# A block of cross attention, self attention and 32 experts on one core: a constant filler operand, the router's root as a power on POOL, and a different split between whole and split weights

## The chip, the core and the metric

The kernel runs on one core of one Trainium2 chip. The metric is the device time of one execution in microseconds. TensorE's matmuls appear as PE in the profile and its weight loads as PEld; VectorE is DVE, ScalarE is ACT, GpSimd is POOL, SyncE is SP.

## The reference

The input x is 4 x 32 rows of 256 numbers, so 128 rows fill the 128 partitions. Three residual steps follow, each on a layer norm of x:

```
x = x + cross_attention(layernorm(x), ctx_512)     # 16 heads, causal: only the first 32 of 512 positions count
x = x + attention(layernorm(x))                    # 16 heads; q, k, v, o are W x + b plus a rank-16 product, scaled 0.5
x = x + experts(layernorm(x))

experts: scores = sqrt(softplus(h @ router_w.T))            # 128 x 32
         idx    = top 4 of scores + expert_bias
         p      = scores at idx, divided by their sum; 0 elsewhere
         out    = sum over 32 experts of p * (silu(clip(h @ gate.T)) * clip(h @ up.T)) @ down.T
                + the same of one shared expert, with weight 1      # clip to -7..7, inner width 128
```

All of it is computed for every expert; the router's weights are zero for those not chosen. Inputs, weights and output are float32.

## The kernel before, in words

The order of every engine's instructions is written out by hand; semaphores join the engines. x stays in one 128 x 256 tile. Attention comes first, in two passes (`a` = 0 and 1), and then the experts in 16 **pairs** of two. Code and text count pairs 0 to 15; the TensorE functions take n = pair + 1, with n = 0 for the shared expert.

**Whole and split.** A product of float32 operands can be done *whole*, directly from the loaded weights (`gate_up_whole`, `down` for n up to `FIRST`). Or it can be done *split*: the weights are written as a high part in a shorter format plus a low part (the remainder), the activations likewise, and TensorE adds three products of high and low parts (`HI_LO`). Gate and up weights of pairs below `WHOLE` are used whole, the others split. Down weights of the last `LAST` pairs are split, the others whole.

**Who makes the parts.** ACT copies the loaded weights (`gu_raw`, eight slots) to the high part in `gu_w` (`gu_high`, L654 to L659, one pair at a time). POOL subtracts it and writes the low part in halves of 128x512 (`gu_low`, L324 to L329). For down weights the same is done by `dn_high` (L742 to L747) and L337 to L341, which put both parts in slots of `gu_w` that are free by then. `gate_up` for a split pair waits for each half's low part (L555). POOL runs one list: three powers for the layer norms' inverse roots (`inverse_sqrt`), two sums for the merged value weights, then the low parts. It waits for the last shift of the second attention (L322) before the first low part, and after four halves for the third inverse root and for the gate (L333 to L335).

**The opening.** TensorE starts with `WARM` = 9 matmuls on a tile of ones (`keep_busy`, L416 to L420), which DVE sets first (L834). Some more of these stand in the attention.

**The router.** From the logits ACT and DVE take absolute value, exponential, logarithm and a ratio to softplus (L714 to L720 and L912 to L920). The square root is then made by ACT as exp(ln / 2) (L723 and L726) and refined by one division and sum on DVE (L927 to L934), so `score2` is twice the root. DVE adds the bias to get the key (L935), finds the top eight, marks the chosen ones, sums and divides (L937 to L942): this is the gate. ACT loads the table for silu behind the exponential (L727). DVE's `clip` of the shared expert and of pair 0 stands between these steps (L923, L929).

**The expert loop** (L613 to L622 on TensorE) does, for n from 2 to 16: `gate_up(n + 4)`, the transposes of n, `down(n - 2)`. DVE clips (L900), ACT applies silu (L734), DVE multiplies with up and the gate (`gate_h`, L953), TensorE transposes, ACT copies (`hT_unit`, L740), and for split downs DVE makes the low part (`hT_low`, L966). ACT has one gu conversion per round.

**Loads.** SP issues nearly all loads in one order (L254 to L285): attention's, gu 4, 5, 6, 0, shared, 1, 2, 3, 7, down 0 to 3, and then gu and down in turn. gu 8 to 11 wait for both low halves of pairs 4 to 7, gu 12 to 15 for TensorE's whole products, since they reuse slots.

Of the kernel before, what the change touches and what calls it, by code (L numbers as in the profile page):

```python
# [12 lines left out]
BF16 = mybir.dt.bfloat16  # L13
# [6 lines left out]
T = B * S  # L20
# [17 lines left out]
WHOLE = 4  # L38
LAST = 6
# [3 lines left out]
TINY = 1e-30  # L43

# [11 lines left out]
def raw_slot(p):  # L56
    return p if p < RAW else (p - WHOLE) % RAW


def build(nc, x, consts, mask, small, ctx_kv, x_wq, lora, rows, attn_w, shared_w, moe_w, out):  # L60
    with ExitStack() as ctx:
# [46 lines left out]
        ln_floor = sb("ln_floor", [T, 1])  # L108
# [20 lines left out]
        warm_sb = sb("warm_sb", [128, 128], BF16)  # L129
# [8 lines left out]
        ln_softplus = sb("ln_softplus", [T, E])  # L138
        half_power = sb("half_power", [T, E])
        root = sb("root", [T, E])  # L140
        inv_root = sb("inv_root", [T, E])
        score2 = sb("score2", [T, E + 1])
# [29 lines left out]
        warm_set = sem("warm_set")  # L172
# [54 lines left out]
        ln_softplus_ready = sem("ln_softplus_ready")  # L227
        half_power_ready = sem("half_power_ready")
        root_ready = sem("root_ready")
# [22 lines left out]
        @block.sync  # L252
        def _(sp):
            for name, dst, src in (("x", x_sb[:], x), ("xwq", xwq_sb[:], x_wq), ("mask", mask_sb[:], mask), ("lora", lora_sb[:], lora),  # L254
                                   ("aw_kq", aw_sb[:, 0:2], attn_w[:, 0:2]), ("small", small_sb[:], small),
                                   ("aw_vo", aw_sb[:, 2:4], attn_w[:, 2:4]), ("rows", bo_rows[:], rows.to_broadcast([T, D]))):
                sp.dma_start(dst, src).then_inc(ld[name], 16)

            def load_gu(p):
                if p >= RAW + WHOLE:  # L260
                    sp.wait_ge(gu_ready, p - RAW - WHOLE + 2)
                elif p >= RAW:
                    for c in range(DC):
                        sp.wait_ge(gu_lo_ready[c], p - RAW + 1)
                sp.dma_start(gu_raw[:, raw_slot(p)], moe_w[:, p * PAIR:p * PAIR + DC * GU]).then_inc(ld_gu[p], 16)

            def load_dn(p):
                sp.dma_start(dn_w[:, p * 2 * D:(p + 1) * 2 * D], moe_w[:, p * PAIR + DC * GU:(p + 1) * PAIR]
                             ).then_inc(ld_dn[p], 16)

            load_gu(WHOLE)
            load_gu(WHOLE + 1)
            load_gu(WHOLE + 2)
            load_gu(0)
            sp.dma_start(shared_sb[:], shared_w).then_inc(ld["shared"], 16)
            for p in range(1, WHOLE):
                load_gu(p)
            load_gu(WHOLE + 3)
            for p in range(WHOLE):
                load_dn(p)  # L280
            for p in range(RAW, PAIRS):
                load_gu(p)
                load_dn(p - RAW + WHOLE)
            for p in range(PAIRS - RAW + WHOLE, PAIRS):
                load_dn(p)  # L285
            sp.wait_ge(fin, 1)
            sp.dma_start(out, x_sb[:]).then_inc(stored, 16)
            sp.wait_ge(stored, 16)

        @block.gpsimd  # L290
        def _(pool):
            nc.gpsimd.memset(minus_mean[:], -1.0 / D).then_inc(powers_set, 1)
            nc.gpsimd.memset(inv_sqrt_power[:], -0.5).then_inc(powers_set, 1)
            nc.gpsimd.memset(ln_floor[:], 2.0 ** -64).then_inc(powers_set, 1)
            nc.gpsimd.memset(v_heads[:], 0.0).then_inc(zeroed, 1)
            nc.gpsimd.memset(key[:, E:E + K], SENTINEL).then_inc(zeroed, 1)
            nc.gpsimd.memset(score2[:, E:E + 1], 2e-20).then_inc(zeroed, 1)
# [46 lines left out]
        def _(pe):  # L344
# [265 lines left out]
            gate_up(WHOLE + 1)  # L610
# [16 lines left out]
        def _(act):  # L627
# [26 lines left out]
            def gu_high(p):  # L654
# [4 lines left out]
                nc.scalar.activation(gu_w[:, p % SLOTS, 0], gu_raw[:, raw_slot(p)], ACT.Copy).then_inc(gu_hi_ready, 1)  # L659
# [21 lines left out]
            gu_high(WHOLE)  # L681
            act.wait_ge(xt_psum, 1)
# [17 lines left out]
            gu_high(WHOLE + 1)  # L700
# [3 lines left out]

            act.wait_ge(xt_psum, 3)
# [5 lines left out]
            nc.scalar.activation(xnT_parts[:, 0], xfT[:], ACT.Copy).then_inc(xt_hi_ready, 1)  # L711
            act.wait_ge(rstd_ready[2], 1)
# [8 lines left out]
            act.wait_ge(softplus_ready, 1)  # L721
            act.wait_ge(powers_set, 3)
# [43 lines left out]
        def _(dve):  # L766
# [67 lines left out]
            nc.vector.memset(warm_sb[:], 1.0).then_inc(warm_set, 1)  # L834
# [73 lines left out]
            for w, bound in enumerate((CLIP, -CLIP)):  # L908
# [8 lines left out]
            step(nc.vector.tensor_tensor(den[:], den[:], e_abs[:], ALU.mult))  # L917
# [20 lines left out]
            step(nc.vector.match_replace(replaced[:], top8[:], key[:], -SENTINEL))  # L938
            step(nc.vector.scalar_tensor_tensor(weight[:], replaced[:, 0:E + 1], -SENTINEL, score2[:],
# [104 lines left out]
```

## Time and profile before

| | |
|---|---|
| time of the runs | 74.11, 76.31, 76.15 us; median 76.15 |
| profiled execution | 74.17 us, its span 72.2 us |
| PE / PEld busy | 67.5 us / 49.4 us |
| DVE, ACT, POOL busy | 44.7, 40.9, 42.9 us |
| bytes read from HBM | 15.52 MB |

The span runs from the first to the last instruction of the profiled execution; the time of an execution has a little more around it. The views used below are the page's busy line, its groups of instructions, the chain of waits in order of time, the timeline, and the DMA issues of a window with their time to landing. Times in the timeline and in the chain are counted from the span's start.

### The profile page before, as it was taken

What the parts mean: (1) busy time and instruction counts of PE and PEld (TensorE: products, weight loads), DVE (VectorE), ACT (ScalarE), POOL (GpSimd) and SP (SyncE); (2) the same over time, 40 slices, a digit from 0 to 9 for tenths busy, and PEclk for the clock granted to TensorE, in tenths of its full rate; (3) what the DMA queues carried; (4) which work ended last, traced back from release to release, by engine and by line L of the source; (5) the groups of instructions that cost most, each with busy time, mean ns of one, the idle gap of its engine ahead of it and who ended that gap; (6) DMA issues with size and microseconds to landing.
All of it is one profiled execution on the core that took longest, in us unless ns stands there. A gap on an engine that the chain in (4) does not pass through costs nothing.

```text
span 72.2 us, 1555 instructions
## 1 busy us (share of the span) xinstructions
PE 67.5 (93%) x552; PEld 49.4 (68%) x552; DVE 44.7 (62%) x126; ACT 40.9 (57%) x88; POOL 42.9 (59%) x50
## 2 busy tenths in 40 slices
PE   4999998999999999999999999999999999998950
PEld 1337565797864495644686888887888888897940
DVE  0058587684697627598999936634753574589520
ACT  0604556375449440459969968868960366696300
POOL 7330006150009973000799999999999999999200
PEclk9999999999999999999999999999999999999999
DMA  0899999999999499800006999999990000000002
GB/s 5 276 295 267 375 331 378 390 417 417 412 402 386 161 265 315 328 15 5 0 0 159 318 354 385 397 395 415 382 365 25 9 0 0 0 0 0 0 0 73
DMA packets 6342, 15.74 MB, mean 218 GB/s; under 512 B 704, under 2 KB 1472, under 8 KB 6336
## 3 DMA queue, kind: packets, MB, share of 16 engines
q1 hardware_dynamic: 6048, 15.39, 59.5%
q10 hardware_dynamic: 288, 0.27, 1.1%
q8 instruction: 4, 0.07, 0.3%
q14 instruction: 2, 0.02, 0.1%
HBM read 15.52 MB, written 0.13 MB: 217 GB/s over the span
## 4 chain that ended last, share of the span: by engine, by line
PE 68%; DVE 15%; ACT 9%; issue 4%; POOL 1%; DVEq 0%; ACTq 0%
PE bP L557 15%; PE bY L579 11%; PE bE L419 6%; PE bXT L569 5%; PE bP L356 4%; PE bY L587 4%; PE bE L557 4%; DVE gu_clip L900 3%; PE bY L408 3%; PE bXT L412 3%; PE bP L383 2%; DVE h L953 2%; DVE shifted L795 2%; ACT L727 2%; DVE row_max L793 2%
## 5 line engine op out<-in xcount | busy, mean ns | idle before, releaser
L328 POOL TENSOR_TENSOR gu_w<-gu_raw,gu_w 128x512 fp32r<-128x512 f32 x24 | 29.9, 1281 | 11.5 <-DVE gate L942 6.0
L557 PE MATMUL bP<-gu_w,xnT_parts 128*128 128x512 f32 x60 | 17.6, 428 | 0.0
L900 DVE TENSOR_SCALAR gu_clip<-bP,clip_at 128x512 f32<-128x512 f32 x13 | 10.4, 808 | 7.7 <-PE bP L557 7.7
L659 ACT ACTIVATE gu_w<-gu_raw 128x1024 fp32r<-128x1024 f32 x12 | 12.7, 1055 | 3.0 <-DMA gu_raw<-moe_w_dram 2.9
L557 PEld LDWEIGHTS bP<-gu_w,xnT_parts 128*128 128x128 f32 x60 | 11.2, 188 | 2.7 <-issue 0.5
L579 PE MATMUL bY<-dn_w,hT 128*128 128x256 f32 x40 | 10.3, 380 | 0.0
L953 DVE SCALAR_TENSOR_TENSOR h<-gu_clip,gate,bP 128x128 f32<-128x128 f32 x26 | 7.8, 340 | 0.5 <-ACT bP L734 0.4
L340 POOL TENSOR_TENSOR gu_w<-dn_w,gu_w 128x512 fp32r<-128x512 f32 x6 | 7.5, 1276 | 0.0
L579 PEld LDWEIGHTS bY<-dn_w,hT 128*128 128x128 f32 x40 | 6.8, 190 | 0.5
L740 ACT ACTIVATE hT<-bXT 128x256 f32<-128x256 f32 (+1 forms) x11 | 4.0, 366 | 4.8 <-PE bXT L569 4.8
L569 PE MATMUL bXT<-consts_sb,h 128*128 128x128 f32 x33 | 6.3, 275 | 0.3 <-DVE hT_parts L966 0.2
L734 ACT ACTIVATE bP<-gu_clip,rstd 128x256 f32<-128x256 f32 x13 | 6.1, 471 | 0.0
L569 PEld LDWEIGHTS bXT<-consts_sb,h 128*128 128x128 f32 x33 | 4.3, 140 | 2.5 <-DVE h L953 0.9
L419 PE MATMUL bE<-warm_sb 128*128 128x512 bf16 x12 | 5.0, 569 | 1.0 <-DVE warm_sb L834 1.0
L543 PE MATMUL bP<-gu_raw,xfT 128*128 128x512 f32 x12 | 5.7, 599 | 0.0
L316 POOL TENSOR_TENSOR aw_sb<-aw_sb,lora_v 128x256 f32<-128x256 f32 x2 | 1.4, 730 | 6.4 <-ACT lora_v L651 6.4
L587 PE MATMUL bY<-gu_w,hT_parts 128*128 128x256 f32 x36 | 5.2, 289 | 0.0
L308 POOL TENSOR_TENSOR rstd<-var_eps,inv_sqrt_power 128x1 f32<-128x1 f32 x3 | 1.8, 599 | 5.5 <-DVE var_eps L780 5.5
L587 PEld LDWEIGHTS bY<-gu_w,hT_parts 128*128 128x128 f32 x36 | 4.5, 189 | 0.0
L788 DVE TENSOR_TENSOR k_heads<-bP,consts_sb 128x512 f32<-128x512 f32 x4 | 2.7, 689 | 2.1 <-PE bP L426 1.1
L900 DVE TENSOR_SCALAR gu_clip<-bE,clip_at 128x512 f32<-128x512 f32 x3 | 2.4, 807 | 2.3 <-PE bE L557 2.3
L740 ACT ACTIVATE hT_parts<-bXT 128x256 fp32r<-128x256 f32 x6 | 2.3, 380 | 2.5 <-PE bXT L569 2.5
(151 smaller groups left out, 105.8 us busy)
## 6 DMA issues: line engine op xcount, KB each, us to landing
gu_raw<-moe_w_dram SPq DMA_DIRECT2D x16, 512.0 KB, 9.0
dn_w<-moe_w_dram SPq DMA_DIRECT2D x16, 256.0 KB, 8.2
aw_sb<-attn_w_dram SPq DMA_DIRECT2D x2, 512.0 KB, 7.1
shared_sb<-shared_w_dram SPq DMA_DIRECT2D x1, 384.0 KB, 12.3
small_sb<-small_dram SPq DMA_DIRECT2D x1, 370.0 KB, 7.0
xwq_sb<-x_wq_dram SPq DMA_DIRECT2D x1, 256.0 KB, 3.5
lora_sb<-lora_dram SPq DMA_DIRECT2D x1, 256.0 KB, 4.4
ctx_sb<-ctx_kv_dram ACTq DMA_DIRECT2D x1, 192.0 KB, 3.0
```

Source lines behind the costliest of these rows:

```text
L328: nc.gpsimd.tensor_tensor(gu_w[:, p % SLOTS, 1, cols], gu_raw[:, raw_slot(p), cols], gu_w[:, p % SLOTS, 0, cols], ALU.subtract).then_inc(g ...
L340: nc.gpsimd.tensor_tensor(dn_part(i, 1), dn_w[:, at:at + 2 * D], dn_part(i, 0), ALU.subtract).then_inc(dn_lo_ready, 1)
L419: nc.tensor.matmul(bank, warm_sb[:], warm_sb[:].unsqueeze(1).to_broadcast([128, 4, 128]), start=True, stop=True, skip_group_check=True)
L557: last = nc.tensor.matmul(bGU[n % 5][:, 0:GU], xnT_parts[:, a, k, :], gu_w[:, (n - 1) % SLOTS, w, k * GU:(k + 1) * GU], start=(k == 0 and ...
L569: last = nc.tensor.transpose(bHT[n % 2][:, e * T:(e + 1) * T], h[:, n % 4, e, :], ident)
L579: last = nc.tensor.matmul(bY[:, 0:D], hT[:, n % 3, e, :], dn_w[:, at:at + D], start=False, stop=False, skip_group_check=True)
L587: last = nc.tensor.matmul(bY[:, 0:D], hT_parts[:, n % 3, a, e, :], dn_part(i, w)[:, e * D:(e + 1) * D], start=False, stop=(n == PAIRS and ...
L659: nc.scalar.activation(gu_w[:, p % SLOTS, 0], gu_raw[:, raw_slot(p)], ACT.Copy).then_inc(gu_hi_ready, 1)
L734: nc.scalar.activation(dst, gu_clip[:, n % 4, 0:width, 0, :], ACT.Silu, scale=rstd[:, 2:3]).then_inc(silu_ready, 1)
L740: nc.scalar.activation(dst, bHT[n % 2][:, 0:width * T], ACT.Copy).then_inc(hT_ready, 1)
L900: nc.vector.tensor_scalar(gu_clip[:, n % 4, 0:width], bank[:, 0:width * 2 * I], clip_at[:, 0:1], clip_at[:, 1:2], ALU.min, ALU.max).then_i ...
L953: last = nc.vector.scalar_tensor_tensor(h[:, n % 4, e], gu_clip[:, n % 4, e, 1, :], weight_e, bank[:, e * 2 * I:e * 2 * I + I], ALU.mult, ...
```

## The change

Five things change.

1. The filler matmuls take constants that the program has anyway (a column of ones, broadcast) in place of the tile that DVE set.
2. The root is one `pow` with exponent 0.5 on POOL. ACT's second logarithm and second exponential and DVE's half_power, reciprocal, product and sum go. `score` is the root itself, not twice the root. POOL's wait for the gate stands right behind it.
3. `WHOLE` goes from 4 to 2: pairs 2 and 3 are split too. ACT makes the high parts of pairs 2 to 6 and one half of pair 7 ahead of the router, some in halves (`gu_high_chunk`). POOL doesn't wait for the shift any more and does nine halves, not four, before the third inverse root. In the loop ACT is one conversion further ahead (`EARLY` = 9).
4. `LAST` goes from 6 to 8: eight down products are split.
5. SP's order of loads changes; the `rows` load moves behind two gu loads.

```
-WHOLE = 4
-LAST = 6
+WHOLE = 2
+EARLY = 9
+LAST = 8
+SMALLEST = 2e-38
 def raw_slot(p):
-    return p if p < RAW else (p - WHOLE) % RAW
+    return p if p < RAW else (p + WHOLE) % RAW
...
+        ones = nc.const_aps.tensor(1.0, [128, 128], BF16)
+        ones_wide = nc.const_aps.tensor(1.0, [128, 512], BF16)
...
@@ SP: loads
-                if p >= RAW + WHOLE:
-                    sp.wait_ge(gu_ready, p - RAW - WHOLE + 2)
+                if p >= 2 * RAW - WHOLE:
+                    sp.wait_ge(gu_ready, p - 2 * RAW + WHOLE + 2)
...
             load_gu(WHOLE)
             load_gu(WHOLE + 1)
-            load_gu(WHOLE + 2)
+            sp.dma_start(bo_rows[:], rows.to_broadcast([T, D])).then_inc(ld["rows"], 16)
+            for p in range(WHOLE + 2, RAW - 1):
+                load_gu(p)
             load_gu(0)
+            load_gu(RAW - 1)
             sp.dma_start(shared_sb[:], shared_w).then_inc(ld["shared"], 16)
-            for p in range(1, WHOLE):
+            load_gu(1)
+            for p in range(RAW, RAW + 4):
+                load_dn(p - RAW)
                 load_gu(p)
-            load_gu(WHOLE + 3)
-            for p in range(WHOLE):
+            for p in range(4, 8):
                 load_dn(p)
-            for p in range(RAW, PAIRS):
+            for p in range(2 * RAW - WHOLE, PAIRS):
                 load_gu(p)
-                load_dn(p - RAW + WHOLE)
-            for p in range(PAIRS - RAW + WHOLE, PAIRS):
+            for p in range(RAW + 4, 2 * RAW - WHOLE):
+                load_gu(p)
+            for p in range(8, PAIRS):
                 load_dn(p)
@@ POOL
-            pool.wait_ge(shift_ready, 2 * DC)
             def gu_low(p, c):
-                pool.wait_ge(gu_hi_ready, p - WHOLE + 1)
+                pool.wait_ge(gu_hi_ready, DC * (p - WHOLE) + c + 1)
...
-                    if (p, c) == (WHOLE + 2, 0):
+                    if (p, c) == (WHOLE + 4, 1):
                         inverse_sqrt(2)
+                        pool.wait_ge(softplus_ready, 1)
+                        nc.gpsimd.tensor_tensor(score[:, 0:E], softplus[:], half[:], ALU.pow).then_inc(score_ready, 1)
                         pool.wait_ge(gate_ready, 1)
@@ TensorE
-                    nc.tensor.matmul(bank, warm_sb[:], warm_sb[:].unsqueeze(1).to_broadcast([128, 4, 128]),
+                    nc.tensor.matmul(bank, ones, ones_wide,
...
-            pe.wait_ge(warm_set, 1)
...
             pe.wait_ge(xt_lo_ready, 1)
-            gate_up(WHOLE + 1)
+            for n in range(WHOLE + 1, 6):
+                gate_up(n)
@@ ACT
+            def gu_high_chunk(p, c):
+                act.wait_ge(ld_gu[p], 16)
+                cols = slice(c * GU, (c + 1) * GU)
+                nc.scalar.activation(gu_w[:, p % SLOTS, 0, cols], gu_raw[:, raw_slot(p), cols], ACT.Copy
+                                     ).then_inc(gu_hi_ready, 1)
             gu_high(WHOLE)
+            gu_high_chunk(WHOLE + 1, 0)
             act.wait_ge(xt_psum, 1)
             nc.scalar.activation(xcT[:, 0], bXT0[:, 0:T], ACT.Copy).then_inc(xt0_ready, 1)
...
+            gu_high_chunk(WHOLE + 1, 1)
...
+            gu_high(WHOLE + 2)
             exp_half(1, 0)
...
             copy_probsT(1)
-            gu_high(WHOLE + 1)
+            gu_high(WHOLE + 3)
...
+            gu_high_chunk(WHOLE + 4, 0)
...
+            gu_high_chunk(WHOLE + 4, 1)
+            gu_high_chunk(WHOLE + 5, 0)
             act.wait_ge(rstd_ready[2], 1)
...
-            nc.scalar.activation(ln_softplus[:], softplus[:], ACT.Ln, bias=ln_floor[:]
-                                 ).then_inc(ln_softplus_ready, 1)
-            act.wait_ge(half_power_ready, 1)
-            nc.scalar.activation(root[:], half_power[:], ACT.Exp, scale=0.5).then_inc(root_ready, 1)
             nc.scalar.preload_act_table(ACT.Silu)
...
-            gu_high(WHOLE + 2)
+            gu_high_chunk(WHOLE + 5, 1)
             silu_unit(0)
             silu_unit(1)
-            gu_high(WHOLE + 3)
+            for p in range(WHOLE + 6, EARLY + 1):
+                gu_high(p)
...
-                if n + 3 + WHOLE < PAIRS:
-                    gu_high(n + 3 + WHOLE)
+                if EARLY + n < PAIRS:
+                    gu_high(EARLY + n)
@@ DVE
-            nc.vector.memset(warm_sb[:], 1.0).then_inc(warm_set, 1)
...
-            step(nc.vector.tensor_tensor(den[:], den[:], e_abs[:], ALU.mult))
+            step(nc.vector.scalar_tensor_tensor(den[:], e_abs[:], SMALLEST, den[:], ALU.max, ALU.mult))
...
-            dve.wait_ge(ln_softplus_ready, 1)
-            nc.vector.scalar_tensor_tensor(half_power[:], logits_sb[:], -100.0, ln_softplus[:], ALU.max, ALU.min
-                                           ).then_inc(half_power_ready, 1)
             clip(1)
-            dve.wait_ge(root_ready, 1)
-            step(nc.vector.reciprocal(inv_root[:], root[:]))
-            step(nc.vector.tensor_tensor(inv_root[:], inv_root[:], softplus[:], ALU.mult))
             dve.wait_ge(zeroed, 3)
-            step(nc.vector.tensor_tensor(score2[:, 0:E], inv_root[:], root[:], ALU.add))
-            step(nc.vector.scalar_tensor_tensor(key[:, 0:E], score2[:, 0:E], 0.5, small_sb[:, EBIAS:EBIAS + E],
-                                                ALU.mult, ALU.add))
+            dve.wait_ge(score_ready, 1)
+            step(nc.vector.tensor_tensor(key[:, 0:E], score[:, 0:E], small_sb[:, EBIAS:EBIAS + E], ALU.add))
```

## Rows read from the trace of the kernel before

**Rows 1.** The page's busy time, share of the span and instructions of each engine.

```profile
PE 67.5 (93%) x552; PEld 49.4 (68%) x552; DVE 44.7 (62%) x126; ACT 40.9 (57%) x88; POOL 42.9 (59%) x50
```

**Rows 2.** Chain of waits, opening and router: start us, us, what.

```profile
1.04 4.02 PE bE L419 x9
...
31.59 0.14 DVE half_power L927
...
32.00 1.28 ACT L727
```

**Rows 3.** Timeline, opening: start us, us, engine, line, operation [idle before, releaser].

```profile
0.82 0.17 DVE L834 MEMSET warm_sb<- 128x128 bf16 x1 [0.82 <-PEq L1037]
```

**Rows 4.** Timeline of the router stretch, DVE and POOL.

```profile
27.80 0.15 DVE L780 TENSOR_SCALAR var_eps<-moments 128x1 f32<-128x1 f32 x1
...
30.95 0.19 DVE L920 SCALAR_TENSOR_TENSOR softplus<-logits_sb,ratio 128x32 f32<-128x32 f32 x1
...
31.63 0.81 DVE L900 TENSOR_SCALAR gu_clip<-bP,clip_at 128x512 f32<-128x512 f32 x1
...
33.19 0.19 DVE L935 SCALAR_TENSOR_TENSOR key<-score,small_sb 128x32 f32<-128x32 f32 x1
...
34.76 24.97 POOL L328 TENSOR_TENSOR gu_w<-gu_raw,gu_w 128x512 fp32r<-128x512 f32 x20 [6.05 <-DVE gate L942]
```

**Rows 5.** Timeline, TensorE's weight loads around the first pairs, and POOL's last parts.

```profile
31.23 0.19 PEld L543 LDWEIGHTS bP<-gu_raw,xfT 128*128 128x128 f32 x1 [0.24 <-issue]
...
32.95 0.19 PEld L543 LDWEIGHTS bE<-gu_raw,xfT 128*128 128x128 f32 x1 [0.24 <-issue]
...
38.45 0.20 PEld L569 LDWEIGHTS bXT<-consts_sb,h 128*128 128x128 f32 x2 [0.51 <-DVE h L953]
...
59.69 7.49 POOL L340 TENSOR_TENSOR gu_w<-dn_w,gu_w 128x512 fp32r<-128x512 f32 x6
```

**Rows 6.** Chain of waits, the first expert round and the end.

```profile
39.33 1.41 PE bP L557 x6
40.73 0.22 PE bXT L569 x2
40.95 0.86 PE bY L579 x4
...
63.59 1.15 ACT gu_w L746 x2
...
66.63 0.71 PE bY L587 x6
...
67.55 2.12 PE bY L587 x18
```

**Rows 7.** Timeline of the second half of attention, POOL, ACT and DVE.

```profile
15.88 0.38 POOL L320 TENSOR_SCALAR bo_centred<-consts_sb,bo_mean 128x2 f32<-128x2 f32 x1
...
15.98 0.28 ACT L683 ACTIVATE xcT<-bXT 128x128 f32<-128x128 f32 x1 [0.43 <-PE bXT L486]
...
16.63 0.42 DVE L867 TENSOR_TENSOR xnT<-xcT,bY 128x256 f32<-128x256 f32 x1
...
20.74 0.42 ACT L636 ACTIVATE probs<-shifted 128x256 f32<-128x256 f32 x1 [1.18 <-DVE shifted L795]
...
22.93 1.05 ACT L659 ACTIVATE gu_w<-gu_raw 128x1024 fp32r<-128x1024 f32 x1
```

**Rows 8.** The page's groups: POOL's subtractions, sums and powers | busy us, mean ns | idle before.

```profile
L328 POOL TENSOR_TENSOR gu_w<-gu_raw,gu_w 128x512 fp32r<-128x512 f32 x24 | 29.9, 1281 | 11.5 <-DVE gate L942 6.0
...
L316 POOL TENSOR_TENSOR aw_sb<-aw_sb,lora_v 128x256 f32<-128x256 f32 x2 | 1.4, 730 | 6.4 <-ACT lora_v L651 6.4
...
L308 POOL TENSOR_TENSOR rstd<-var_eps,inv_sqrt_power 128x1 f32<-128x1 f32 x3 | 1.8, 599 | 5.5 <-DVE var_eps L780 5.5
```

**Rows 9.** DMA issues at 4.46 and 5.28 us: KB, us from issue to landing.

```profile
gu_raw<-moe_w_dram SPq DMA_DIRECT2D x1, 512.0 KB, 10.0
...
gu_raw<-moe_w_dram SPq DMA_DIRECT2D x1, 512.0 KB, 10.5
```

More of the change, by code:

```diff
@@ L107, in build @@
         inv_sqrt_power = sb("inv_sqrt_power", [T, 1])
-        ln_floor = sb("ln_floor", [T, 1])
         xc = sb("xc", [T, D])
@@ L128, in build @@
         heads_outT = sb("heads_outT", [128, 2, DC, T])
-        warm_sb = sb("warm_sb", [128, 128], BF16)
+        ones = nc.const_aps.tensor(1.0, [128, 128], BF16)
+        ones_wide = nc.const_aps.tensor(1.0, [128, 512], BF16)
         logits_sb = sb("logits_sb", [T, E])
@@ L137, in build @@
         softplus = sb("softplus", [T, E])
[L138 to L142, printed above, removed]
+        half = sb("half", [T, E])
+        score = sb("score", [T, E + 1])
         key = sb("key", [T, E + K])
@@ L171, in build @@
         powers_set = sem("powers_set")
-        warm_set = sem("warm_set")
         xc_psum = sem("xc_psum")
@@ L226, in build @@
         softplus_ready = sem("softplus_ready")
-        ln_softplus_ready = sem("ln_softplus_ready")
-        half_power_ready = sem("half_power_ready")
-        root_ready = sem("root_ready")
+        score_ready = sem("score_ready")
         route_step = sem("route_step")
@@ L255, in _ @@
                                    ("aw_kq", aw_sb[:, 0:2], attn_w[:, 0:2]), ("small", small_sb[:], small),
-                                   ("aw_vo", aw_sb[:, 2:4], attn_w[:, 2:4]), ("rows", bo_rows[:], rows.to_broadcast([T, D]))):
+                                   ("aw_vo", aw_sb[:, 2:4], attn_w[:, 2:4])):
                 sp.dma_start(dst, src).then_inc(ld[name], 16)
             def load_gu(p):
-                if p >= RAW + WHOLE:
-                    sp.wait_ge(gu_ready, p - RAW - WHOLE + 2)
+                if p >= 2 * RAW - WHOLE:
+                    sp.wait_ge(gu_ready, p - 2 * RAW + WHOLE + 2)
                 elif p >= RAW:
@@ L293, in _ @@
             nc.gpsimd.memset(inv_sqrt_power[:], -0.5).then_inc(powers_set, 1)
-            nc.gpsimd.memset(ln_floor[:], 2.0 ** -64).then_inc(powers_set, 1)
+            nc.gpsimd.memset(half[:], 0.5).then_inc(powers_set, 1)
             nc.gpsimd.memset(v_heads[:], 0.0).then_inc(zeroed, 1)
             nc.gpsimd.memset(key[:, E:E + K], SENTINEL).then_inc(zeroed, 1)
-            nc.gpsimd.memset(score2[:, E:E + 1], 2e-20).then_inc(zeroed, 1)
+            nc.gpsimd.memset(score[:, E:E + 1], 1e-20).then_inc(zeroed, 1)
             pool.wait_ge(zeroed, 3)
@@ L658, in gu_high @@
                     act.wait_ge(gu_ready, p - SLOTS + 2)
-                nc.scalar.activation(gu_w[:, p % SLOTS, 0], gu_raw[:, raw_slot(p)], ACT.Copy).then_inc(gu_hi_ready, 1)
+                nc.scalar.activation(gu_w[:, p % SLOTS, 0], gu_raw[:, raw_slot(p)], ACT.Copy).then_inc(gu_hi_ready, DC)
+            def gu_high_chunk(p, c):
[3 more added lines that the diff above has]
+                                     ).then_inc(gu_hi_ready, 1)
             for c, done in ((0, xc0_ready), (1, xc1_ready)):
@@ L720, in _ @@
             nc.scalar.activation(ln_one_plus[:], one_plus[:], ACT.Ln).then_inc(ln_ready, 1)
-            act.wait_ge(softplus_ready, 1)
-            act.wait_ge(powers_set, 3)
-            nc.scalar.activation(ln_softplus[:], softplus[:], ACT.Ln, bias=ln_floor[:]
-                                 ).then_inc(ln_softplus_ready, 1)
-            act.wait_ge(half_power_ready, 1)
-            nc.scalar.activation(root[:], half_power[:], ACT.Exp, scale=0.5).then_inc(root_ready, 1)
             nc.scalar.preload_act_table(ACT.Silu)
@@ L923, in _ @@
             clip(0)
-            dve.wait_ge(ln_softplus_ready, 1)
-            nc.vector.scalar_tensor_tensor(half_power[:], logits_sb[:], -100.0, ln_softplus[:], ALU.max, ALU.min
-                                           ).then_inc(half_power_ready, 1)
             clip(1)
-            dve.wait_ge(root_ready, 1)
-            step(nc.vector.reciprocal(inv_root[:], root[:]))
-            step(nc.vector.tensor_tensor(inv_root[:], inv_root[:], softplus[:], ALU.mult))
             dve.wait_ge(zeroed, 3)
-            step(nc.vector.tensor_tensor(score2[:, 0:E], inv_root[:], root[:], ALU.add))
-            step(nc.vector.scalar_tensor_tensor(key[:, 0:E], score2[:, 0:E], 0.5, small_sb[:, EBIAS:EBIAS + E],
-                                                ALU.mult, ALU.add))
+            dve.wait_ge(score_ready, 1)
+            step(nc.vector.tensor_tensor(key[:, 0:E], score[:, 0:E], small_sb[:, EBIAS:EBIAS + E], ALU.add))
             step(nc.vector.max(top8[:], key[:]))
             step(nc.vector.match_replace(replaced[:], top8[:], key[:], -SENTINEL))
-            step(nc.vector.scalar_tensor_tensor(weight[:], replaced[:, 0:E + 1], -SENTINEL, score2[:],
+            step(nc.vector.scalar_tensor_tensor(weight[:], replaced[:, 0:E + 1], -SENTINEL, score[:],
                                                 ALU.is_equal, ALU.mult, accum_out=weight_sum[:, 0:1]))
```

## Prediction

> **What bounds the kernel now.** I read the page's busy line first: TensorE is busy 67.5 of 72.2 us, POOL 42.9 [rows 1]. Shares over a whole span do not say what an edit is worth, so the chain of waits is read next, stretch by stretch.
>
> Opening: nine filler matmuls take 4.02 us of the chain, and the first real matmul comes right behind them [rows 2]. They do 512 columns in 4.02/9 = 0.447 us each, the 1.2 GHz level. The first waits for a DVE set that starts at 0.82 and holds the filler back until 1.04 [rows 2, 3].
>
> Router: the variance is formed at 27.80, softplus starts at 30.95, the key at 33.19, and POOL, which waits for the gate, takes up its low parts at 34.76 [rows 4]. The chain here goes through the root's steps and ACT's table load of 1.28 us [rows 2]. From 34.76 on POOL never pauses: 20 low parts in 24.97 us, then 6 for down weights until 67.18 [rows 4, 5]. TensorE stands still once, up to 0.5 us ahead of the transposes at 38.45, for DVE's h [rows 5].
>
> Experts: from 39.33 TensorE repeats 1.40 us (gate and up of a split pair), 0.22 (transposes) and 0.86 (an unsplit down), 2.48 in all; a split down takes 0.71 [rows 6]. DVE and ACT wait for it. Ten such rounds (24.8), four transpose steps and six split downs (4 x 0.22 + 6 x 0.71 = 5.14) would end at 69.27; the last matmul ends at 69.67 [rows 6]. The 0.40 of stall lie behind two conversions on ACT at 63.59 that hold back the last silus [rows 6]. POOL's last product is there at 67.18, 1.8 us before the last down starts (69.67 - 0.71 = 68.96): POOL has slack now.
>
> **The change, part by part.** The sum is against the profiled execution: 72.2 us of span, 74.17 us of time, 1.97 us around it.
>
> *Opening.* The DVE set goes; the constant it is replaced by is written before the program's own work. TensorE can start where DVE did, at 0.82 instead of 1.04: 0.22 us. Above, 0.3; below, nothing: if the clock rises when it does now, the first products merely run at the slow level. I take 0.20.
>
> *Conversions in attention.* Pairs 2 to 6 and half of 7 are now made high by ACT ahead of the router, in pieces: a whole one 1.05 us [rows 7], a half 1.15/2 = 0.58, like a down weight of its size [rows 6]. The first half needs the second gu load. The first two landed at 4.46 + 10.0 = 14.46 and 5.28 + 10.5 = 15.8 [rows 9]; the 128 KB of rows no longer stand ahead, a quarter of the 1.3 us between them, so 15.5 now. The half ends near 16.1; the copy to xcT (15.98, less 0.20, by itself) then runs 16.1 to 16.4, just before xnT's start at 16.63 - 0.20 = 16.43 [rows 7]. Cost nothing, at worst 0.3 if the load is as late as the second is now. The tightest of the other places is a whole conversion of 1.05 in the 1.18 us that ACT waits before its exponential at 20.74 [rows 7]; what does not fit there comes straight onto the chain.
>
> *POOL in attention.* Its wait for the shift goes. It is free at 15.88 + 0.38 - 0.20 = 16.1 [rows 7] and does nine low parts before the third root, at 24.97/20 = 1.248 us each [rows 4]: 11.2 us, and pair 5's parts can't start before 22.93 + 1.05 - 0.20 = 23.8 [rows 7], where the seventh part would stand at 23.6. So the ninth ends at 27.5. The variance is ready at 27.80 + 0.15 - 0.20 = 27.75: the third root is not late, by 0.2 us. Cost nothing.
>
> *Root.* Removed: ACT's logarithm and exponential, and on DVE half_power, a reciprocal and the products around it; added: one power on POOL, 128x32. DVE now goes softplus, clip 0, clip 1, key. Clip 1 starts at 31.63 less half_power's 0.14 [rows 2] less 0.20 = 31.29 and takes 0.81 [rows 4]: the key can start at 32.10 instead of 33.19, **1.09 us earlier**. POOL can start the power at 31.0 (softplus ends at 31.14 - 0.20). So a power of up to 1.0 us is hidden behind the two clips. Its price: the trace has only 128x1, 0.60 us; a plain 128x256 costs 0.73 and a 128x512 1.28 [rows 8], which is 2.15 ns a column and 0.18 fixed. Lower end 0.60 + 31 x 0.00215 = 0.67. Upper end, if all over 0.18 is paid per column: 0.18 + 32 x 0.42 = 13.6. I take at most 1.0, since 32 columns of the same operation are nearer to its row of one column than to a cost that grows thirty-twofold. It is the weakest step, and both ends are kept.
>
> The Trainium skill (GPSIMD Engine Reference, section Elementwise, side-by-side cycle accounting) puts a two-input element at about 2.6 cycles, which the 2.15 ns bear out, and data-dependent branching at about 12 cycles an element at 1.2 GHz. By that the power would be 0.60 + 0.32 = 0.9 us, an estimate from that page, and the time the forecast's; by the rows' upper end it would be the slower rival's.
>
> *Table load.* It goes ahead of softplus on ACT, which has then nothing to do until clip 0 is through. The 1.28 us leave the chain.
>
> *Two pairs split instead of whole.* A whole pair takes 1.72 us (weight loads at 31.23 and 32.95 begin two of them [rows 5]), a split one 1.40: 0.64 off TensorE. It was ready for the transposes of 2 at 38.45 - 0.51 = 37.94 [rows 5]; now at 37.94 - 0.20 - 0.64 = 37.10. h comes with the gate, at 38.45 - 1.09 = 37.36. A stall of 0.3 stays, and 1.09 us are gained here, the three parts together.
>
> *Two more down products split.* 2 x (0.86 - 0.71) = 0.30 off TensorE. ACT's last conversions now fall in round 11, ahead of the last silus, so the 0.40 of stall goes. TensorE's end: 69.67 - 1.09 - 0.30 - 0.40 = 67.88.
>
> *What is late next.* POOL has 28 + 8 = 36 parts instead of 30; nine are done before the gate, 27 stand behind it where 26 did. It starts at 34.76 - 1.09 = 33.67 and ends at 33.67 + 27 x 1.248 = 67.37; the last down is 0.71 more, with 0.05 for the signal: **68.13**. That is later than 67.88, so POOL sets the end. Gain 69.67 - 68.13 = 1.5 us.
>
> *DMA.* gu loads 8 to 11 wait for low parts that are done between 18.6 and 26.4 and are sent while the queue is still full; 14 and 15 wait for products that are through at 31.2 [rows 5]; 12 waits for the tenth part, 34.9, and is converted some 5 us later. In the queue the down loads 0 to 7 now come earlier, 8 to 15 last, for products after 50 us. Cost nothing, covered by several us.
>
> Sum: 74.17 - 1.5 = **72.6 us**, 2.1% less. The median of the runs shown, 76.15, lies 1.98 over the profiled execution (the lowest, 74.11, with it). A median of the new kernel that fell as high would be 74.6.
>
> **Rivals.**
> *The power costs more than its cover, in part.* Each us over 1.0 moves gate, h and POOL's 27 parts alike: at 2.0 us 73.6, at 2.5 the gain is gone. For it: one column costs 0.42 over a plain one. Against: that may be fixed. 0.23.
> *The power is paid per column: slower.* Place: POOL between softplus and key. It decides from 2.5 us on, beyond 2% from 4.0 us. At the upper end of 13.6 us the gate comes 12.6 later: 85.2 us. Against it: that a loop over 32 columns would overlap nothing. 0.13.
> *A cover in attention fails,* or the opening brings nothing: the first half, the conversion before the exponential or the third root late by 0.2 to 0.6 us: about 73.1. For it: margins of 0.0 to 0.2. 0.13.
> *More than forecast.* The opening gives 0.3 and POOL's parts follow closer, so that TensorE sets the end: 67.8, time 72.3 or below. 0.06.
> The forecast itself, 72.3 to 72.9: 0.45.
>
> **How the numbers follow.** About 2% (1.5 us) is what a measurement can tell from no change; faster is below 72.7. The forecast straddles it, more below than above (0.34), the last rival adds 0.06, the first 0.02: 0.42. Same: the rest of the forecast, most of the first rival, the third: 0.46. Slower 0.12. The range goes from 71.8 (TensorE's end and the opening's unknowns) to 75.0, which holds a power of up to 3.4 us and a median at 74.6; the dear power stays out.
>
> **What would show it.** First filler at 0.8; xnT at 16.4; nine low parts from 16.1 to 27.5, third root at 27.8; power at most 1.0 us, key at 32.1, POOL's next part at 33.7; transposes of 2 at 37.4; rounds of 2.48 without a gap; POOL's last part at 67.4 and the last six matmuls behind it. A power over 1 us, a third root after 28, or gaps on TensorE between 40 and 60 us would make it wrong.

## The result: 4.3% slower, and the profile after

The changed kernel takes 77.76 us in the median of five runs (76.74 to 79.17), the kernel before 74.11 (73.70 to 76.31, also five runs; the three listed ahead are among them). In some executions of every kernel here the time is about 3 or 7% longer (the changed kernel's profiled one, 79.17 us, is such a one), and the ratios leave these out. The ratio is **1.043, interval 1.037 to 1.049**. The forecast was 72.6 us, in a range up to 75.0; slower had a chance of 0.12.

The page's busy line, to set beside [rows 1]:

```profile
PE 70.0 (91%) x558; PEld 52.8 (68%) x560; DVE 44.3 (57%) x123; ACT 43.7 (57%) x93; POOL 55.8 (72%) x57
```

POOL is busy 12.9 us more. Six more low parts are 6 x 1.25 = 7.5; the other 5.4 are one instruction. The page's groups of POOL, to set beside [rows 8]:

```profile
L328 POOL TENSOR_TENSOR gu_w<-gu_raw,gu_w 128x512 fp32r<-128x512 f32 x28 | 34.8, 1280 | 2.1 <-DVE gate L943 1.7
...
L336 POOL TENSOR_TENSOR score<-softplus,half 128x32 f32<-128x32 f32 x1 | 5.4, 5438 | 2.3 <-DVE softplus L928 2.3
```

The chain of waits (start us, us, what), to set beside [rows 2, 6]:

```profile
0.76 4.00 PE bE L421 x9
4.76 1.15 PE bP L427 x4
...
32.63 5.45 POOL score L336
...
41.17 2.56 PE bP L558 x6
...
44.39 1.41 PE bP L558 x6
...
72.10 2.32 PE bY L588 x18
```

The power stands on the chain with its whole 5.45 us. The timeline of the same stretch, to set beside [rows 4, 5, 7]:

```profile
17.87 7.43 POOL L328 TENSOR_TENSOR gu_w<-gu_raw,gu_w 128x512 fp32r<-128x512 f32 x6
...
18.28 0.42 DVE L875 TENSOR_TENSOR xnT<-xcT,bY 128x256 f32<-128x256 f32 x1
...
25.70 3.72 POOL L328 TENSOR_TENSOR gu_w<-gu_raw,gu_w 128x512 fp32r<-128x512 f32 x3 [0.41 <-ACT gu_w L661]
...
29.68 0.68 POOL L309 TENSOR_TENSOR rstd<-var_eps,inv_sqrt_power 128x1 f32<-128x1 f32 x1 [0.25 <-DVE var_eps L789]
...
32.93 0.80 DVE L908 TENSOR_SCALAR gu_clip<-bP,clip_at 128x512 f32<-128x512 f32 x1
...
38.17 0.19 DVE L937 TENSOR_TENSOR key<-score,small_sb 128x32 f32<-128x32 f32 x1 [4.44 <-POOL score L336]
...
39.74 23.65 POOL L328 TENSOR_TENSOR gu_w<-gu_raw,gu_w 128x512 fp32r<-128x512 f32 x19 [1.67 <-DVE gate L943]
39.97 0.33 PE L570 MATMUL bXT<-consts_sb,h 128*128 128x128 f32 x1 [2.31 <-DVE h L954]
...
63.33 10.05 POOL L342 TENSOR_TENSOR gu_w<-dn_w,gu_w 128x512 fp32r<-128x512 f32 x8
```

DVE has both clips done at 33.73 and then waits 4.44 us for the power. TensorE stands still for 2.31 us, and its first six products behind that take 2.56 us instead of 1.41: the granted clock is 0.52 from 41.17 to 43.73 us, the lower of the two levels (1.2 GHz), and 1.00 again from 43.73 on. In the kernel before, where TensorE hardly stood still (below), it stays at 1.00.

**A ruler.** The absolute times hold something that is not the change. In this profile the first products are slow: from the end of the nine fillers to the end of the eight products of L358, 4.78 us pass, where the kernel before needed 2.73 (1.15 and 0.69 for the first four). The durations are those of the lower clock level, by a factor of 1.83 for the eight (2.00 us against 1.09), as in the stretch above; the granted clock in the rows says 1.00 for both and doesn't show it. From one profiled execution to the next this moves all that follows by up to 2 us. So I compare traces from the start of the third inverse root to the end of the last matmul. The kernel before (chain, timeline):

```profile
5.06 0.69 PE bP L426 x4
...
28.03 0.68 POOL L308 TENSOR_TENSOR rstd<-var_eps,inv_sqrt_power 128x1 f32<-128x1 f32 x1 [1.31 <-DVE var_eps L780]
```

Before it is 69.67 - 28.03 = 41.64 us; the forecast was 68.13 - 27.83 = 40.3; now it is 74.42 - 29.68 = **44.74, 3.1 more** (the root starts 3.0 us ahead of the power). Of 74.11 us that is 4.2%, next to the 4.3% of the times.

### The profile page after: what moved, and what is told of

Same layout as the page of the kernel before. It is cut to its first block, busy times and chain, and to the rows that moved or that the text cites. A ratio compares the mean times of both kernels' runs of the same rounds, so it can differ in the third digit from the quotient of the medians.

```text
span 77.3 us, 1587 instructions
## 1 busy us (share of the span) xinstructions
PE 70.0 (91%) x558; PEld 52.8 (68%) x560; DVE 44.3 (57%) x123; ACT 43.7 (57%) x93; POOL 55.8 (72%) x57
## 4 chain that ended last, share of the span: by engine, by line
PE 72%; DVE 10%; POOL 8%; issue 5%; ACT 1%; DVEq 0%; POOLq 0%
PE bP L558 18%; PE bY L580 9%; PE bY L588 8%; POOL score L336 7%; PE bE L421 5%; PE bXT L570 5%; PE bP L358 5%; PE bE L558 4%; PE bY L410 3%; PE bXT L414 2%; PE bP L385 2%; DVE shifted L804 2%; DVE row_max L802 2%; PE bP L427 1%; PE bY L367 1%
## 5 line engine op out<-in xcount | busy, mean ns | idle before, releaser
L328 POOL TENSOR_TENSOR gu_w<-gu_raw,gu_w 128x512 fp32r<-128x512 f32 x28 | 34.8, 1280 | 2.1 <-DVE gate L943 1.7
L558 PE MATMUL bP<-gu_w,xnT_parts 128*128 128x512 f32 x66 | 20.2, 445 | 0.0
L558 PEld LDWEIGHTS bP<-gu_w,xnT_parts 128*128 128x128 f32 x66 | 13.1, 201 | 3.1 <-issue 0.5
L661 ACT ACTIVATE gu_w<-gu_raw 128x1024 fp32r<-128x1024 f32 x11 | 11.4, 1047 | 0.4 <-issue 0.4
L342 POOL TENSOR_TENSOR gu_w<-dn_w,gu_w 128x512 fp32r<-128x512 f32 x8 | 10.1, 1305 | 0.0
L580 PE MATMUL bY<-dn_w,hT 128*128 128x256 f32 x32 | 8.2, 380 | 0.0
L588 PE MATMUL bY<-gu_w,hT_parts 128*128 128x256 f32 x48 | 7.2, 292 | 0.0
L336 POOL TENSOR_TENSOR score<-softplus,half 128x32 f32<-128x32 f32 x1 | 5.4, 5438 | 2.3 <-DVE softplus L928 2.3
L421 PE MATMUL bE<-const-bfloat16-1.0 128*128 128x512 bf16 x12 | 5.0, 565 | 0.8 <-PEq L1038 0.8
L558 PE MATMUL bE<-gu_w,xnT_parts 128*128 128x512 f32 x18 | 5.1, 416 | 0.0
L754 ACT ACTIVATE gu_w<-dn_w 128x512 fp32r<-128x512 f32 x8 | 4.6, 624 | 0.0
```

The costliest lines, as they stand in the source:

```text
L336: nc.gpsimd.tensor_tensor(score[:, 0:E], softplus[:], half[:], ALU.pow).then_inc(score_ready, 1)
L342: nc.gpsimd.tensor_tensor(dn_part(i, 1), dn_w[:, at:at + 2 * D], dn_part(i, 0), ALU.subtract).then_inc(dn_lo_ready, 1)
L421: nc.tensor.matmul(bank, ones, ones_wide, start=True, stop=True, skip_group_check=True)
L558: last = nc.tensor.matmul(bGU[n % 5][:, 0:GU], xnT_parts[:, a, k, :], gu_w[:, (n - 1) % SLOTS, w, k * GU:(k + 1) * GU], start=(k == 0 and ...
L580: last = nc.tensor.matmul(bY[:, 0:D], hT[:, n % 3, e, :], dn_w[:, at:at + D], start=False, stop=False, skip_group_check=True)
L588: last = nc.tensor.matmul(bY[:, 0:D], hT_parts[:, n % 3, a, e, :], dn_part(i, w)[:, e * D:(e + 1) * D], start=False, stop=(n == PAIRS and ...
```

## Experiments

**1. The old root in the changed kernel.**

```
-    nc.gpsimd.tensor_tensor(score[:, 0:E], softplus[:], half[:], ALU.pow)
+    ACT: Ln of softplus, Exp with scale 0.5; DVE: half_power, reciprocal, product, sum    # as before
```

> The changed kernel with the old root put back (ACT's second logarithm and exponential, DVE's division and sum, no power on POOL); constant filler, WHOLE = 2, EARLY = 9, LAST = 8 and the new order of loads stay. Theory 'price of the power': the power took 5.44 us where 1.0 was hidden, and all else works as forecast. Then the gate stands where it stood before less the opening's 0.2 us, POOL starts its 27 parts behind it at 34.76 - 0.2 = 34.56, ends at 68.26, and the last matmul ends near 69.0 against 69.67: about 73.5 us, ratio to the kernel before about 0.99. Rival 'the rest is slow': the nine early low parts, the pieces on ACT in the attention or the six additional parts on POOL delay the chain by themselves; then it stays at 76 us or above, ratio over 1.02.

Measured: 73.69 us, ratio **0.993 (0.989 to 0.997)**. The theory's 0.99 holds; the rival falls: the rest of the change is no loss, it is a small gain. The end of the chain of waits:

```profile
36.38 23.71 POOL gu_w L334 x19
...
65.08 5.01 POOL gu_w L346 x4
...
70.14 0.99 PE bY L592 x6
```

From the gate on the chain is POOL alone, with the last six matmuls behind it. The third root starts at 29.89, so the ruler reads 71.12 - 29.89 = 41.23. The last down after such a wait costs 1.03 us, not the 0.76 that I had taken from back-to-back ones.

**2. The power alone in the kernel before.**

```
-    ACT: Ln, Exp; DVE: half_power, reciprocal, product, sum
+    nc.gpsimd.tensor_tensor(score[:, 0:E], softplus[:], half[:], ALU.pow)    # WHOLE 4, LAST 6 stay
```

> The kernel before with the root alone changed to one power on POOL; WHOLE = 4, LAST = 6, the old loads and the old filler tile stay. Theory 'price of the power': POOL is busy with it from 31.2 to 36.65, the key starts at 36.7 instead of 33.19, 3.5 us late, and TensorE's chain with it: 77.7 us, and up to 1.2 more if TensorE's clock falls in the idle time (78.9); ratio 1.047 to 1.064. Rival 'the rest is slow': the power costs little here, 74 to 75 us, ratio under 1.015.

Measured: 78.37 us, ratio **1.051 (1.045 to 1.058)**, in the theory's band; the rival falls. Timeline of POOL:

```profile
30.25 0.68 POOL L303 TENSOR_TENSOR rstd<-var_eps,inv_sqrt_power 128x1 f32<-128x1 f32 x1 [1.32 <-DVE var_eps L771]
33.45 5.44 POOL L331 TENSOR_TENSOR score<-softplus,half 128x32 f32<-128x32 f32 x1 [2.53 <-DVE softplus L911]
40.56 24.91 POOL L323 TENSOR_TENSOR gu_w<-gu_raw,gu_w 128x512 fp32r<-128x512 f32 x20 [1.67 <-DVE gate L926]
```

The ruler reads 45.39, 3.75 over the kernel before. With experiment 1 the change falls into two parts: the power costs 44.74 - 41.23 = 3.5 us, and the rest, without what it gains in the opening, gives 41.64 - 41.23 = 0.4. Of this 0.4, 0.25 go with the filler's operand (experiment 9).

**3. What a power costs by width.** Eight instructions at the end of POOL's list in the kernel before (shortened):

```
+    for cols, op in ((1, pow), (2, pow), (4, pow), (8, pow), (16, pow), (32, pow), (64, pow), (32, add)):
+        nc.gpsimd.tensor_tensor(sweep_out[:, 0:cols], sweep_in[:, 0:cols], sweep_half[:, 0:cols], op)
```

> The kernel before with eight more instructions at the end of POOL's list, on constants in tiles of their own: powers of 1, 2, 4, 8, 16, 32 and 64 columns and a sum of 32 columns. Theory 'price per column': the two measured powers (0.56 us for 1 column, 5.44 for 32) give 0.157 us a column and 0.40 fixed, so 0.56, 0.72, 1.03, 1.66, 2.9, 5.4 and 10.5 us; the sum about 0.25. Rival 'fixed cost or first use': the 5.44 us are mostly a price paid once or in steps, and the wide ones here cost far less than 5 us. Theory 'nothing overlapped', the upper end of the prediction: 0.42 us a column, 13.6 us for 32.

Measured (groups by shape in narrow windows: busy us, mean ns | idle before; the last row's 251 ns is the sum; 2, 4 and 8 columns took 702, 1012 and 1635):

```profile
L351 POOL TENSOR_TENSOR sweep_out<-sweep_in,sweep_half 128x1 f32<-128x1 f32 x1 | 0.6, 554 | 0.1
...
L351 POOL TENSOR_TENSOR sweep_out<-sweep_in,sweep_half 128x16 f32<-128x16 f32 x1 | 2.9, 2898 | 0.1
...
L351 POOL TENSOR_TENSOR sweep_out<-sweep_in,sweep_half 128x32 f32<-128x32 f32 x1 | 5.4, 5426 | 0.1
...
L351 POOL TENSOR_TENSOR sweep_out<-sweep_in,sweep_half 128x64 f32<-128x64 f32 x1 | 10.5, 10546 | 0.1
...
L351 POOL TENSOR_TENSOR sweep_out<-sweep_in,sweep_half 128x32 f32<-128x32 f32 x1 | 0.3, 251 | 0.1
```

A straight line: (5426 - 554)/31 = 157 ns a column and 0.40 us fixed; from 32 to 64 columns it is 160 ns. So there is a price per column, 73 times the 2.15 ns of a plain one. It is not a price of first use, and not the 0.42 us of the prediction's upper end, which took all that one column cost over a plain one for a price per column.

**4. The power on 4 of 32 columns in the changed kernel.** This is the kernel with the price that the prediction had assumed. It leaves out 28 of the 32 roots (these scores are a constant), so it is of use for its time alone.

```
-    nc.gpsimd.tensor_tensor(score[:, 0:E], softplus[:], half[:], ALU.pow)
+    nc.gpsimd.tensor_tensor(score[:, 0:4], softplus[:, 0:4], half[:, 0:4], ALU.pow)
```

> The changed kernel with the power on only 4 of the 32 columns; the other scores are a constant, so 28 of 32 roots are left out. The sweep priced this width at 1.03 us, the size that the prediction had assumed for all 32. Theory 'price of the power': everything else works as forecast, so the key follows clip 1 at once, near 31.7 us when the third root starts at 27.6, POOL starts at 33.2 and ends at 66.9, and the last matmuls 1.0 us later: 72.4 us, ratio to the kernel before about 0.977. Rival 'the rest costs something too': the time stays at the level of the kernel with the old root, 73.7 us, ratio 0.993.

Measured: 73.06 us against 74.43, ratio **0.985 (0.978 to 0.992)**. Timeline of POOL, the end of the chain of waits, and the last weight loads:

```profile
27.84 0.68 POOL L309 TENSOR_TENSOR rstd<-var_eps,inv_sqrt_power 128x1 f32<-128x1 f32 x1 [0.25 <-DVE var_eps L789]
30.80 1.02 POOL L336 TENSOR_TENSOR score<-softplus,half 128x4 f32<-128x4 f32 x1 [2.27 <-DVE softplus L928]
33.49 23.70 POOL L328 TENSOR_TENSOR gu_w<-gu_raw,gu_w 128x512 fp32r<-128x512 f32 x19 [1.67 <-DVE gate L943]
57.14 10.03 POOL L342 TENSOR_TENSOR gu_w<-dn_w,gu_w 128x512 fp32r<-128x512 f32 x8
```

```profile
65.89 2.32 PE bY L588 x18
```

```profile
67.22 0.77 PEld L588 LDWEIGHTS bY<-gu_w,hT_parts 128*128 128x128 f32 x6 [0.15 <-POOL gu_w L342]
```

Third root at 27.84 (forecast 27.8), POOL's next part at 33.49 (33.67), its last at 67.17 (67.37), the last matmul at 68.21 (68.13). The ruler reads 40.37 against a forecast of 40.3. With a power of 1.0 us the sum of the rest is right to 0.1 us. Two small misses cancel in it: POOL is 0.2 us early, and the last down behind its last part takes 1.04 us, not 0.76. By the time alone the run decides nothing: the theory's 0.977 lies just below the interval and the rival's 0.993 just above it. The trace decides.

**5. Does the fallen clock cost anything?** 11 fillers ahead of the transposes that wait for h:

```
+            pe.wait_ge(abs_ready, 1)
+            pe.wait_ge(softplus_ready, 1)
+            keep_busy(11, bLogits[:])
             transpose_h(0, width=1)
```

> The changed kernel with 11 filler matmuls of 512 columns ahead of the first transposes of h, where TensorE stood idle for 2.3 us while the gate was late. Theory 'clock': the fall of the granted clock behind this idle time costs 1.15 us on the first products after it (2.56 us where 1.41 is usual), and the kernel gains that much against the changed kernel: about 75.6 us, ratio to the kernel before about 1.027. Rival 'POOL is the second bound': the products become fast again, but POOL's 27 parts behind the gate end at the same time and the last down needs 0.76 us more, so that of 1.15 us only 0.3 arrive: about 76.5 us, ratio about 1.038.

Measured: 77.38 us, ratio 1.039 (1.032 to 1.045), which the changed kernel's own interval overlaps. The end of its chain:

```profile
71.34 0.99 PE bY L588 x6
```

The products became fast again: the granted clock is 1.00 from 37.8 to 42 us, behind the late h. But the ruler reads 72.33 - 27.57 = 44.76, the changed kernel's 44.74. The clock theory falls; POOL holds the end. The 2.56 us of slow products are real and cost nothing, since POOL's 27 parts behind the late gate end no earlier.

**6 to 8. POOL without its wait for the gate.** With the old root, with the power, and with the power and the fillers:

```
                        inverse_sqrt(2)
-                       pool.wait_ge(gate_ready, 1)
```

> The changed kernel with the old root and without POOL's wait for the gate: POOL goes on with its parts right behind the third inverse root. Theory 'POOL sets the end': in the kernel with the old root the last six matmuls wait for POOL. Here POOL is held only by ACT's second half of pair 7 (33.2 us in a run whose third root starts at 27.6) and ends near 64.4, so TensorE sets the end at about 68.1 instead of 68.8: 72.9 us, ratio to the kernel before about 0.98. Rival 'POOL beside the router': its parts, now beside DVE's small router steps, slow these by the ports that both share, the gate comes later and the gain is lost: ratio 0.993 or more.

> The changed kernel, power and all, without POOL's wait for the gate. POOL starts its 27 parts 1.65 us earlier and is no bound any more. Theory 'clock hidden behind POOL': TensorE then sets the end, with the 1.15 us that its slow first products cost still in it; only about 0.2 us are gained on the changed kernel: about 76.6 us, ratio 1.040. Rival 'POOL alone': the whole 1.65 us arrive: 75.2 us, ratio 1.02.

> Both together: 11 filler matmuls while TensorE waits for the gate and no wait for the gate on POOL. Theory 'clock hidden behind POOL': with POOL out of the way, keeping TensorE busy now pays the 1.15 us that it did not pay alone: about 75.4 us, ratio to the kernel before about 1.024, and 1.1 us under the run without fillers. Rival 'no price of the clock': the same as without the fillers, ratio 1.04.

Measured: with the old root 74.97 us, ratio **1.014 (1.007 to 1.020)** where 0.98 was expected; with the power 80.88 us in the median of six and 79.27 at the lowest, a ratio of 1.07 to 1.09, where I had 1.02 or 1.04; with fillers too 78.95, 1.065 (1.058 to 1.072). All three are misses, and the rival 'POOL beside the router' is right. The timeline with the old root, first with the wait (experiment 1), then without it:

```profile
30.60 0.23 DVE L927 SCALAR_TENSOR_TENSOR clip_at<-var_eps,rstd 128x1 f32<-128x1 f32 x2 [0.44 <-POOL rstd L315]
...
31.51 0.18 DVE L933 TENSOR_SCALAR den<-one_plus 128x32 f32<-128x32 f32 x1 [0.34 <-ACT one_plus L736]
...
36.00 0.30 DVE L960 TENSOR_SCALAR gate<-weight,weight_sum,rstd 128x32 f32<-128x32 f32 x1
```

```profile
27.96 2.48 POOL L334 TENSOR_TENSOR gu_w<-gu_raw,gu_w 128x512 fp32r<-128x512 f32 x2
...
28.02 1.28 DVE L926 SCALAR_TENSOR_TENSOR clip_at<-var_eps,rstd 128x1 f32<-128x1 f32 x2 [0.44 <-POOL rstd L315]
...
29.23 0.24 DVE L929 TENSOR_SCALAR logits_sb<-bXT,rstd 128x32 f32<-128x32 f32 x1
...
29.51 0.98 DVE L932 TENSOR_SCALAR den<-one_plus 128x32 f32<-128x32 f32 x1
...
34.41 1.28 POOL L334 TENSOR_TENSOR gu_w<-gu_raw,gu_w 128x512 fp32r<-128x512 f32 x1 [3.97 <-ACT gu_w L669]
...
34.59 0.16 DVE L958 RECIPROCAL weight_sum<-weight_sum 128x1 f32<-128x1 f32 x1
...
34.78 0.95 DVE L959 TENSOR_SCALAR gate<-weight,weight_sum,rstd 128x32 f32<-128x32 f32 x1
```

Two `clip_at` steps took 0.23 us before and now 1.28, `den` 0.18 and now 0.98, the gate 0.30 and now 0.95. Each is over only when the POOL subtraction beside it is (two end at 29.2 and 30.4, one at 35.7). In the run with the power the key does the same, 0.19 to 1.17, and the weights, 0.20 to 0.67; the top eight between them is not held up:

```profile
38.02 7.40 POOL L328 TENSOR_TENSOR gu_w<-gu_raw,gu_w 128x512 fp32r<-128x512 f32 x6
38.15 1.17 DVE L936 TENSOR_TENSOR key<-score,small_sb 128x32 f32<-128x32 f32 x1 [4.45 <-POOL score L336]
39.36 0.20 DVE L937 MAX8 top<-key 128x8 f32<-128x36 f32 x1
...
39.88 0.67 DVE L939 SCALAR_TENSOR_TENSOR weight<-replaced,score 128x33 f32<-128x33 f32 x1
```

`logits_sb`, which reads PSUM, and the one-column reciprocal are not held up either, though a subtraction runs beside them. So POOL's wait for the gate keeps its long subtractions away from those of the router's steps from SBUF to SBUF that they hold up. The rulers: 42.65 without the wait and with the old root, against 41.23 with it; 47.32 and, with fillers, 47.02 with the power, against 44.74. The medians of the last two runs lie 1.9 us apart, by the ruler the fillers give 0.3; the rest lies ahead of the third root (29.66 us in one profile, 27.27 in the other). The last run doesn't price the clock, though. Its fillers end at 37.7 us, TensorE then stands still for 2.0 us until the late h, and the granted clock is 0.52 from 41 to 44 us all the same. What a kept clock is worth with POOL out of the way stays open.

**9. The constant filler alone in the kernel before.**

```
-            pe.wait_ge(warm_set, 1)
-            nc.vector.memset(warm_sb[:], 1.0).then_inc(warm_set, 1)
```

> The kernel before with only the fillers' operand changed to the program's constant, no DVE set. The prediction took 0.20 us for it: the first filler at 0.8 instead of 1.04 and all that follows as much earlier, ratio 0.997. Rival 'more': in two profiles of kernels with the constant the third root started at 27.3 to 27.6 instead of 28.03, so the clock also rises earlier in relation to the real work: 0.45 us or more, ratio 0.994. Rival 'nothing': the rise of the clock, not the first filler, sets the pace of the first products: ratio 1.000.

Measured: ratio 0.995 (0.991 to 0.999). That is between the 0.20 us of the prediction and the rival's 0.45, and excludes neither. The trace shows a second gain, which no expectation named. In the kernel before, DVE pauses for 0.27 us ahead of the reciprocal in the softplus; here it doesn't (timeline, before and then this run):

```profile
30.11 0.35 DVE L916 RECIPROCAL den<-den 128x32 f32<-128x32 f32 x1 [0.27 <-DVE den L915]
```

```profile
30.02 0.35 DVE L914 RECIPROCAL den<-den 128x32 f32<-128x32 f32 x1
```

So POOL resumes 6.48 us behind the third root and not 6.73, and the ruler reads 41.39 and not 41.64. The pause stands in the three kernels whose DVE program begins with the set (before, experiments 2 and 3) and in none of the nine without it; why, no run shows. In its profiled execution the gain of the opening was lost again at ACT's first conversion, which waited for the first gu load, 10.98 us after its issue (10.0 in [rows 9]):

```profile
4.46 10.98 DMA gu_raw<-moe_w_dram
...
15.46 1.06 ACT gu_w L658
```

**10. A version that beats both: old root, seven split downs.**

```
-LAST = 8
+LAST = 7
```

ACT's conversions of down weights, two a round, are written so that an odd number is possible.

> The changed kernel with the old root and LAST = 7: seven down products split instead of eight, so POOL has 26 parts behind the gate instead of 27. Theory 'POOL sets the end with the old root': one part less frees 1.25 us on POOL and costs TensorE 0.15, so the end moves by about 0.6 us, until TensorE sets it: 0.6 us under the kernel with the old root and LAST = 8, ratio to the kernel before about 0.985. Rival 'TensorE sets the end': the unsplit product costs 0.15 us and the time stays or rises: ratio 0.993 to 0.996.

Measured: 73.36 us against 74.09, ratio **0.988 (0.981 to 0.994)**, where 0.985 was expected. Timeline of POOL, and the end of the chain of waits, which is now TensorE's:

```profile
34.22 23.68 POOL L334 TENSOR_TENSOR gu_w<-gu_raw,gu_w 128x512 fp32r<-128x512 f32 x19 [5.82 <-DVE gate L960]
57.87 8.75 POOL L346 TENSOR_TENSOR gu_w<-dn_w,gu_w 128x512 fp32r<-128x512 f32 x7
```

```profile
66.32 2.12 PE bY L592 x18
```

The ruler reads 68.44 - 27.73 = 40.71, 0.52 under the kernel with eight split downs, where 0.6 was expected. POOL's last part is there at 66.62 and no longer holds anything up. Removing work from TensorE (the eighth split down, 0.15 us) had cost more on POOL than it gave. That this beats eight split downs rests on the traces; the intervals of the two ratios overlap.

## Why the prediction was wrong

**The step that failed** is the price of the power: "I take at most 1.0, since 32 columns of the same operation are nearer to its row of one column than to a cost that grows thirty-twofold". It is 5.44 us. That reasoning chose between two ends 13 us apart by nearness in name, not by a slope. The row of one column held a surcharge of 0.42 us over a plain one, and I had nothing that said which part of it was fixed. The two bounds did contain the value. The later expectations, worked out from two measured widths, met those two and the six other numbers within 0.05 us.

**The Trainium skill's rule** went with the wrong side. The Trainium skill (GPSIMD Engine Reference, section Elementwise, side-by-side cycle accounting) gives about 12 cycles an element for data-dependent branching, from which I estimated 0.9 us. The measured 157 ns a column are 188 cycles at the 1.2 GHz that the Trainium skill gives (GPSIMD Engine Reference, section Specifications). The first of these sections says nothing of a power; I used its rule as if it did. Its 2.6 cycles for a plain two-input element agree with the 2.15 ns a column of the prediction.

**The slower rival** was the right one, in mechanism and place: POOL between softplus and key, beyond 2% from 4.0 us on. At 5.44 the rule of the rival beside it (each us over 1.0 moves gate, h and 27 parts alike) gives 72.6 + 4.4 = 77.0 us; five runs gave 76.74 to 79.17, and between experiment 4 and the changed kernel 4.42 us more of power moved the ruler by 4.37. It had 0.13, with a price per column of 0.42 us, 2.7 times what was measured. Together with "dearer in part" a power beyond its cover had 0.36, though the one row there was could not tell a fixed surcharge from a price per column.

**Right:** xnT is not late (its start lies 11.4 us ahead of the third root in the changed kernel, as before); the nine low parts end 0.25 us ahead of the third root. Experiment 4 shows the rest: with the cover large enough POOL resumes 5.65 us behind the root (5.84 forecast, 6.73 before), does its 27 parts at 1.25 us each, TensorE does its rounds of 2.48 without a gap, and both end together. The first filler starts 0.28 us sooner than before (0.20 forecast).

**Off in size:** the last down behind a wait for POOL costs 1.03 us, not 0.76 (experiments 1, 4 and 5). POOL's 0.19 us of earliness in experiment 4 is the pause in the softplus that is gone with DVE's set (experiment 9). Both were unforeseen and offset each other, so the 0.1 us of experiment 4 is in part luck. Of the 0.40 us of stall near TensorE's end 0.18 stay: one pair of transposes takes 0.40 us and not 0.22 in the changed kernel and in experiment 4.

**Misread:** TensorE did not stand still for 0.5 us ahead of the transposes at 38.45. The 0.51 us in [rows 5] are idle time of the weight loads; of the 0.95 us from 37.50 to 38.45 PE is busy for 0.89. So it was ready near 38.4, and less 0.20 and 0.64 at 37.55, where it comes to these transposes in experiment 4, with h already there and no stall. The forecast had it ready at 37.10 and waiting 0.3 us for h. The gain in the rounds' start is 1.13 us (38.20 against 39.33), close to the 1.09 that had been taken from h.

**Not seen:** behind TensorE's wait of 2.31 us the granted clock is 0.52 for 2.6 us. It costs nothing as long as POOL sets the end (experiment 5).

## What to carry to other kernels

Before an operation is moved to another engine, find its price per column, not its price: two widths give it, one width never does, and a short instruction's duration can be all overhead or all work. Where two engines end together, as POOL and TensorE here, work taken off one by giving it to the other moves the end only as far as the second one's slack (experiment 10). A wait that seems to hold an engine back for nothing may keep it off a shared path: try it away before believing that it is slack.

## What the runs showed of the hardware

A power on POOL costs about 0.40 us and 157 ns for each column of 128 partitions (148 from the first to the second, 160 from 32 to 64), whether on softplus values or on a constant (5.44 and 5.43 us for 32). One column is not always 0.55 us: the third inverse root takes 0.68 in the traces of both kernels, where the first two take about 0.55. DVE's xnT_parts, with two inputs in SBUF, runs beside it; whether that is the reason was not tested.

A DVE instruction that reads and writes SBUF alone can be held until the POOL subtraction beside it ends: 0.18 to 0.98 us, 0.19 to 1.17, 0.30 to 0.95, 0.20 to 0.67, and 0.23 to 1.28 for the two `clip_at` steps together. Not all are: the top eight (0.20 us), the replacement (0.18) and the one-column reciprocal (0.16) ran beside a subtraction at their usual length. The Trainium skill (GPSIMD Engine Reference, section Specifications) says that POOL shares its SBUF interfaces with VectorE and that they conflict where a DVE instruction has two SBUF inputs or runs in a 2-port mode; the key, the weights and `clip_at` (two SBUF inputs) agree, and so do the logits, whose input is in PSUM and which are not slowed. `den` and the gate have one tensor input; that they ran in such a mode no row shows. In each of these rows the hold lasted until a whole POOL instruction was through.
